# Windowed attention: scores in plain fp32 on 64x64 pieces over three blocks of 64 keys, and the value product on 64x64 pieces into two banks

## The reference

```python
q = l2norm(q) * qs
k = l2norm(k) * ksc
q, k = rotary_xpos(q, k)
...
bq = q.reshape(b, h, w, WINDOW, d) * QK_SCALE
bk, bv = (look_around(bk), look_around(bv))     # the window before, then the own window
sim = jnp.einsum('bhwid,bhwjd->bhwij', bq, bk)
mask = (i < j) | (i > j + WINDOW) | (j == -1)
sim = jnp.where(mask, -jnp.finfo(sim.dtype).max, sim)
attn = jax.nn.softmax(sim, axis=-1)
out = jnp.einsum('bhwij,bhwjd->bhwid', attn, bv)
```

## Time and profile before

| | |
|---|---|
| device time, median of 3 runs | 2664.02 us (2662.18 to 2664.52) |
| span of the profiled execution | 2660.9 us |
| PE / PEld / DVE / ACT / POOL busy | 98 / 87 / 83 / 67 / 60% of the span |
| mean granted TensorE clock | 0.999 of full speed |
| one sequence, from its first score product (565.22) to the next one's (640.66) | 75.4 us |

### The profile page before, as it was taken

How to read it: one execution, slowest core, us unless ns; L and a number is a source line. 1 busy time by engine, 2 the same in 40 slices (tenths; PEclk the granted TensorE clock), 3 DMA queues, 4 the chain that set the end, 5 groups by cost and what they waited for, 6 DMA issues and landing times.

```text
span 2660.9 us, 67491 instructions
## 1 busy us (share of the span) xinstructions
PE 2606.0 (98%) x23392; PEld 2307.9 (87%) x23392; DVE 2215.5 (83%) x6597; ACT 1777.2 (67%) x4872; POOL 1588.3 (60%) x1767
## 2 busy tenths in 40 slices
PE   8999999999999999999999999999999999999999
PEld 7888888888888888888767888888888988988888
DVE  8888888888888888888656888888888889888887
ACT  6677677666676666666454767666666666666665
POOL 6666666656666666665213666666666666666655
PEclk9999999999999999999999999999999999999999
DMA  3122111003000000005101000000003100000000
GB/s 120 34 81 77 38 29 53 22 20 116 14 2 2 2 2 25 2 2 200 34 18 33 2 2 2 2 2 2 2 2 116 34 2 18 18 18 18 17 18 25
DMA packets 75904, 81.38 MB, mean 31 GB/s; under 512 B 37552, under 2 KB 61872, under 8 KB 74416
## 3 DMA queue, kind: packets, MB, share of 16 engines
q1 hardware_dynamic: 70176, 75.51, 8.7%
q10 hardware_dynamic: 5392, 1.56, 0.2%
HBM read 49.53 MB, written 26.74 MB: 29 GB/s over the span
## 4 chain that ended last, share of the span: by engine, by line
PE 73%; DVE 14%; issue 5%; ACT 4%; POOL 4%; DMA 1%; SPq 0%; DVEq 0%; POOLq 0%; ACTq 0%
PE bank L1064 13%; PE bank L1066 12%; PE bank L1065 12%; PE bank L1271 9%; PE bank L1159 5%; PE bank L1124 5%; PE bank L1145 5%; PE bank L1100 4%; POOL pr L611 3%; PE bank L1432 2%; DVE t L1603 2%; DVE t L1600 2%; DVE pr L1638 2%; DVE h L1710 1%; ACT pr L792 1%
## 5 line engine op out<-in xcount | busy, mean ns | idle before, releaser
L611 POOL TENSOR_TENSOR pr<-pr,rden 128x512 f32<-128x512 f32 (+1 forms) x512 | 473.6, 943 | 424.0 <-DVE rden L1647 423.5
L792 ACT ACTIVATE pr<-pr,nb 128x256 f32<-128x256 f32 (+1 forms) x1024 | 479.1, 470 | 301.2 <-DVE nb L1638 301.2
L1638 DVE CUSTOM_DVE_ANT_0 pr<-bank,maskb,r 128x256 f32<-128x256 f32 (+1 forms) x1024 | 401.3, 445 | 20.7 <-PE bank L1124 8.7
L1064 PE MATMUL bank<-h2T,w 128*128 128x256 f32 x1408 | 408.2, 290 | 6.0 <-DVE qT L1624 1.0
L1065 PE MATMUL bank<-h2T,w 128*128 128x256 f32 x1408 | 395.0, 281 | 0.0
L1066 PE MATMUL bank<-h2T,w 128*128 128x256 f32 x1408 | 394.7, 280 | 0.0
L643 POOL TENSOR_TENSOR uTl<-t,uTh 128x256 fp32r<-128x256 f32 x288 | 219.3, 762 | 216.2 <-ACT uTh L868 215.4
L1728 DVE SCALAR_TENSOR_TENSOR t<-bank,b,t 128x256 f32<-128x256 f32 (+1 forms) x384 | 184.6, 481 | 159.6 <-ACT t L853 118.2
L1064 PE MATMUL bank<-wqkv,hT 128*128 128x512 f32 x768 | 303.7, 396 | 2.4 <-DVE nb L1638 2.4
L1065 PE MATMUL bank<-wqkv,hT 128*128 128x512 f32 x768 | 303.1, 395 | 0.0
L1066 PE MATMUL bank<-wqkv,hT 128*128 128x512 f32 x768 | 301.5, 393 | 0.0
(11 more groups left out here) (237 smaller groups left out, 7061.0 us busy)
## 6 DMA issues: line engine op xcount, KB each, us to landing
wqkv<-wqkv_split SPq DMA_DIRECT2D x18, 512.0 KB, 6.4
w<-w_split SPq DMA_DIRECT2D x3, 2816.0 KB, 10.6
Y<-in_x SPq DMA_DIRECT2D x8, 512.0 KB, 6.6
out<-Y SPq DMA_DIRECT2D x8, 512.0 KB, 3.9
stt<-stt SPq DMA_DIRECT2D x224, 3.0 KB
h<-out SPq DMA_DIRECT2D x7, 512.0 KB, 3.9
out<-h SPq DMA_DIRECT2D x7, 512.0 KB, 2.9
stt<-stt SPq DMA_DIRECT2D x192, 0.0 KB
```

Source lines behind the costliest of these rows:

```text
L611: e.tensor_tensor(pr[:, 2 * j:2 * j + 2, 0:wide], pr[:, 2 * j:2 * j + 2, 0:wide], rden[:, 2 * j:2 * j + 2].unsqueeze(2).to_broadcast([P, 2 ...
L792: last = e.activation(pr[:, hd, 0:wide], pr[:, hd, 0:wide], ACT.Exp, bias=nb[:, hd:hd + 1], scale=-1.0, accum_out=den[:, hd:hd + 1])
L1064: e.matmul(out, left[0], right[0], start=first, stop=False)
L1638: m = e.tensor_tensor_reduce(pr[:, hd, 0:wide], bank[j][:, g * 256:g * 256 + wide], far, r[:, t, 1, place(hd):place(hd) + 1], FAR, ALU.add ...
```

## The change

Tokens of a tile are seen in two halves of 64, and keys in blocks of 64. A query half sees 129 of at most three blocks, so scores, mask, exponential and normalisation are 192 wide for 256 (tiles 1 to 3); tile 0 stays 128 wide. The scores are one plain fp32 product for each piece, with no low parts: `kT` and `qT` are single, `A2_k` and `A2_q` go. Each product takes 64 rows (a head) by 64 columns (a query half) of the array; `kT` holds the eight key blocks in falling order. Per tile there are 24 calls (32 in tile 0), and the keys' order differs between the two heads of a pair and the two query halves. The pair lies side by side in 384 columns of `pr`: the outer two times 128 columns are the main parts, the 128 in the middle hold the edge parts of both heads. So a pair takes 3 transposes of 128 x 128 for 4: 8 for the main parts (`PT`) and 4 for the edge parts (`PTE`), 12 for 16.

The value product works on 64 x 64 pieces: the lower 64 keys of a block pair go to bank 6, the upper 64 to bank 3, so two sums lie in two banks. ScalarE copies the first (`O_first`), VectorE adds the second (`O_add`), into `o_sum`, which takes the place of the queries' low part; high and low part of the result are then made from `o_sum`. `A0` moves ahead of `O` on ScalarE and VectorE, and `fill(2)` behind `A2` on TensorE. `cuts` is new; in tile 0 five W2 products come ahead of the scores, where three stood between their halves. Apart from that, the last product of W2 uses 106 rows for 42.

```diff
-        maskb = sb("maskb", [P, 2, 2, WINDOW], BF16)
+        maskb = sb("maskb", [P, 4 * WINDOW], BF16)
-        qT = sb("qT", [P, HL, PAIRS, P], F32R)
+        qT = sb("qT", [P, HL, PAIRS, P])
+        o_sum = qT[:, 1, :, :].rearrange("p a c -> p (a c)")
-        kT = sb("kT", [P, HL, PAIRS, 2, P], F32R)
+        kT = sb("kT", [P, PAIRS, BLOCKS, HB])
+        def wide(t):
+            return 3 * HB if t else 2 * HB
+        def probs(j, t):
+            pr_j = pr[:, j, 0:6 * HB]
+            return cut(pr_j, 2) if t else cut(pr_j, 3)[:, ::2, :]
...
+            def PTE(L, b, t):
+                n = idx(L, b, t)
+                e.wait_ge(pt_ps, at(pt_ps, 3 * n + 3))
+                halves_of = bank[E_BANK][:, :].rearrange("p (u a c) -> p u a c", u=HEADS // 2, a=2)
+                for a in pair:
+                    for g in pair:
+                        last = e.activation(pTe[64 * a:64 * a + 64, g::2, :], halves_of[64 * g:64 * g + 64, :, a, :], ACT.Copy)
+                last.then_inc(pt_sb, 1)
+            def O_first(L, b, t):
+                n = idx(L, b, t)
+                e.wait_ge(o_lo, at(o_lo, 2 * n))
+                e.wait_ge(pv_ps, at(pv_ps, 2 * n + 2))
+                for i in pair:
+                    cols = slice(2 * P * i, 2 * P * i + 2 * P)
+                    e.activation(o_sum[:, cols], bank[O_BANK[0]][:, cols], ACT.Copy).then_inc(o_first, 1)
...
+                own = BLOCKS - 1 - 2 * t
+                if t:
+                    keys = ((((0, own, 3),), ((0, own, 2), (2, own - 1, 1))), (((1, own, 2), (0, own + 2, 1)), ((0, own - 1, 3),)))
+                else:
+                    keys = ((((0, own, 1), (1, own - 1, 1)),) * 2,) * 2
                 for s_ in range(2):
                     p = 2 * half + s_
+                    for g in range(2):
+                        rows = slice(64 * g, 64 * g + 64)
+                        for a in range(2):
+                            out = cut(bank[2 * half + g][64 * a:64 * a + 64, s_ * 256:s_ * 256 + 256], 4)
+                            for to, block, w in keys[s_][a]:
+                                m = e.matmul(out[:, to:to + w, :], qT[rows, 0, p, HB * a:HB * a + HB], kT[rows, p, block:block + w, :],
+                                             start=True, stop=True, skip_group_check=True)
...
+            def PTE(L, b, t, more):
+                n = idx(L, b, t)
+                if t < NT - 1 or more:
+                    e.wait_ge(v_sb, at(v_sb, n + 2))
+                for j in range(HEADS // 2):
+                    mm = e.transpose(bank[E_BANK][:, j * P:(j + 1) * P], pr[:, j, P:2 * P], ident[:, :])
                 mm.then_inc(pt_ps, 1)
...
+                for j in range(HEADS // 2):
+                    if j % 2 == 0:
+                        e.wait_ge(pt_sb, at(pt_sb, 3 * n + j // 2 + 1))
+                    for g in range(2):
+                        for a in range(2):
+                            mm = product(j, g, a, t - 1 if t and a else t, pTm, 0, j == 0, t == 0 and j == 3)
+                if t:
+                    e.wait_ge(pt_sb, at(pt_sb, 3 * n + 3))
+                    for j in range(HEADS // 2):
+                        for g in range(2):
+                            for a in range(2):
+                                mm = product(j, g, a, t if a else t - 1, pTe, HB * a, False, j == 3)
...
-                        rows = (64 + REST, REST)[i]
+                        rows = 64 + REST
...
-                    cuts = ((0, 9, 12, 12, UNITS), (0, 14, 14, 14, UNITS), (0, 14, 14, 14, UNITS), (0, 11, 11, 11, UNITS))[t]
+                    cuts = ((5, 9, 12, 14, UNITS), (0, 6, 11, 14, UNITS), (0, 6, 11, 14, UNITS), (0, 6, 11, 11, UNITS))[t]
...
+            def O_add(L, b, t):
+                n = idx(L, b, t)
+                for i in pair:
+                    cols = slice(2 * P * i, 2 * P * i + 2 * P)
+                    e.wait_ge(o_first, at(o_first, 2 * n + i + 1))
+                    e.tensor_tensor(o_sum[:, cols], bank[O_BANK[1]][:, cols], o_sum[:, cols], ALU.add).then_inc(o_added, 1)
...
+                    O_add(L, b, t)
+                    if ahead2:
+                        A0(*ahead2)
                     O(L, b, t)
                     if t == 3:
                         H2T(L, b, 0)
-                    if ahead2:
-                        A0(*ahead2)
-                    if ahead:
-                        A2_k(*ahead)
-                    if ahead and t < 3:
-                        A2_q(*ahead)
```

More of the change, by code:

```diff
@@ L1143, in PT @@
                 for g in range(2):
-                    for w in range(2 if t else 1):
-                        mm = e.transpose(bank[bk][:, (2 * g + w) * P:(2 * g + w + 1) * P],
-                                         pr[:, 2 * j + g, w * P:(w + 1) * P], ident[:, :])
+                    mm = e.transpose(bank[PT_BANK[a]][:, (2 * (j % 2) + g) * P:(2 * (j % 2) + g + 1) * P],
+                                     pr[:, j, 2 * g * P:(2 * g + 1) * P], ident[:, :])
+                if j % 2:
+                    mm.then_inc(pt_ps, 1 if t or a == 0 else 2)
@@ L1147, in PT, with PV, product @@
+            def PTE(L, b, t, more):
[4 more added lines that the diff above has]
+                    mm = e.transpose(bank[E_BANK][:, j * P:(j + 1) * P], pr[:, j, P:2 * P], ident[:, :])
                 mm.then_inc(pt_ps, 1)
-            def PV(L, b, t, j):
+            def PV(L, b, t):
                 n = idx(L, b, t)
-                if j == 0:
-                    e.wait_ge(xa_done, at(xa_done, n))
-                e.wait_ge(pt_sb, at(pt_sb, 4 * n + j + 1))
-                for g in range(2):
+                e.wait_ge(xa_done, at(xa_done, n))
+                def product(j, g, a, tile, right, lo, first, last):
@@ L1155, in PV @@
                     hd = 2 * j + g
-                    ws = (0, 1) if t else (0,)
-                    for w in ws:
-                        tile = t if w == t % 2 else t - 1
-                        mm = e.matmul(bank[O_BANK[j // 2]][64 * g:64 * g + 64, j % 2 * P:(j % 2 + 1) * P],
-                                      v[:, tile, hd * DH:(hd + 1) * DH], pT[:, hd, w, :],
-                                      start=(w == 0), stop=(w == ws[-1]))
-                if j % 2:
-                    mm.then_inc(pv_ps, 1)
+                    return e.matmul(bank[O_BANK[a]][64 * g:64 * g + 64, j * P + lo:j * P + lo + right.shape[-1]],
+                                    v[64 * a:64 * a + 64, tile, hd * DH:(hd + 1) * DH], right[64 * a:64 * a + 64, hd, :],
+                                    start=first, stop=last, skip_group_check=True)
@@ L1165, in WO @@
+                mm.then_inc(pv_ps, 2)
             def WO(L, b, t):
@@ L2110, in constants @@
     tab = tab.reshape(NT, P, 4, DH).transpose(1, 0, 2, 3).reshape(P, -1)
-    i, j = np.arange(P)[:, None], np.arange(2 * WINDOW)[None]
-    own = np.where(j[:, :WINDOW] > i, f(FAR), f(0))
-    before = np.where(j[:, :WINDOW] < i, f(FAR), f(0))
-    mask = np.concatenate([own, before, before, own], 1)
+    i, j = np.arange(P)[:, None], np.arange(HB)[None]
+    low, i = i < HB, i % HB
+    above, below = np.where(j > i, f(FAR), f(0)), np.where(j < i, f(FAR), f(0))
+    none = np.zeros((P, HB), f)
+    near, back, edge = np.where(low, above, none), np.where(low, none, below), np.where(low, below, above)
+    mask = np.concatenate([near, back, edge, edge, near, back, near, np.where(low, f(FAR), above)], 1)
     r_, c_ = np.arange(P)[:, None] % 64, np.arange(64)[None]
```

130 lines of the change are left out of this document (56 added, 74 removed).

## The result

| | before | after |
|---|---|---|
| median of the runs | 2663.8 us (4 runs, 2662.2 to 2664.5) | 2702.0 us (4 runs, 2701.0 to 2703.8) |
| profiled execution, its span | 2660.9 us | 2700.6 us |
| TensorE busy in the span | 98% | 94% |
| VectorE busy in the span | 83% | 77% |

A forecast was written before the change was run, and what follows sets the result against it. VectorE's chain to the projection, with only 0.30 us of slack, was taken to bound the kernel despite TensorE's 98%. Tiles 0 to 3 summed +0.6 + 0.1 + 0.1 - 0.6 = +0.2; x32 = +6.4, less 2.4: 2668 us, range 2625 to 2700.

The forecast's parts named there:

- To the first exponential: VectorE loop, from its first score operation to the first exponential: 0.80 us instead of 0.93, from two narrower score operations.
- to the squares: VectorE loop, from first exponential to sum of squares: 4.14 us instead of 4.57, from eight narrower exponentials.
- rotations: VectorE loop, squares and rotations up to the attention output's new work: 5.05 us, unchanged.
- 10.6 as the point from which it counts: Value product ending later than about 10.6 us after the scores' start would make ScalarE's bank 6 copy delay VectorE.
- Two additions, hT and low half: VectorE after the rotation: three operations of 0.33 us ahead of a 0.42 us low half, 1.41 against 0.42.
- 0.06 to the projection: Handover from VectorE's finished low half to the start of TensorE's output projection: 0.06 us.
- Projection to its reader: From the output projection's start to VectorE's operation that reads it: about 1.6 us, then 1.36 to the next scores.
- Tile 0, +0.6: One-window tile: no narrower softmax, only the new work on VectorE's chain, so 0.6 us longer per sequence.
- Tile 3, -0.6: Last tile, to the feed-forward part: narrower GpSimd normalisations bring the squares 1.2 us earlier; 14.55 us for 15.10.
- rival 1: GpSimd truly holds tile 3, its relief is larger: squares at about 4.9 instead of 5.82, 2639 us; chance 0.25.
- TensorE's terms: In two-window tiles: scores some 1.6 us (0.2 less), transposes 0.44 less, value product 1.7 (0.3 less); 0.9 less altogether.
- Rival 2: Four-piece instructions cost 26.5 ns or more whatever their columns, so the value product ends at 10.8; 2690 us, chance 0.23.

## Why the prediction was wrong

The direction was given 0.37, the time lay 2 us outside the range. The mechanism was the forecast's own: TensorE's gain is worth nothing, because VectorE's chain to the projection doesn't get shorter (without the sum the kernel is 114 us faster; without the edge products nothing changes). Its price was too low, step by step:

- To the first exponential 0.80 (measured 665.49 - 664.69 = 0.80), to the squares 4.14 (669.63 - 665.49 = 4.14), rotations 5.05 (5.09). Right. The 0.04 may be ScalarE's copy out of bank 6, 10.66 after the scores' start; I had 10.6 as the point from which it counts.
- Two additions, hT and low half, 1.41, and 0.06 to the projection, 1.47 together: measured 1.94 in tile 1, of it 0.38 the hold-up by GpSimd, and 1.56 in the other tiles. **This is the step that failed most**: I took the low half's duration from one that reads PSUM and asked neither what its new source is nor what GpSimd does beside it. Taking the collision away gave 14.7 us of the 34 missing.
- The remaining 1.55 is seen in tile 0 as well: there the first low half is done at 661.56 and the projection starts 0.14 later, not 0.06. Before, the projection hardly ever waited for it, so no row showed a real handover; I took one that was hidden. 0.08 x 4 x 32 = 10 us.
- Projection to its reader, "about 1.6": measured 1.69. The three numbers in my own line give 1.50 - 0.12 + 0.28 = 1.66, which I rounded down, and it was 668.18 - 666.48 = 1.70 before. From there to the scores 1.31 for 1.36. Together 0.04 x 128 = 5 us.
- Tile 0, +0.6: measured +0.70 in the median, which is the handovers. Three of the first nine sequences took 1.6 to 2.2 us more than before instead of 0.7: in two of them TensorE stood for 0.8 us in the W2 products that now go ahead of the scores, the third is not explained. In the sequence whose tile 1 is shown above, the rotation's last addition (L1661) took 0.88 us instead of 0.69, with GpSimd's normalisation of the keys ending 0.33 into it; in the kernel before, the latter ended 0.02 ahead of it. That happened in 4 sequences.
- Tile 3, -0.6: to the projection -0.26, to the start of the feed-forward part -0.55. Right: the squares come 5.76 after the first score operation, where I had 5.82 and rival 1 had 4.9, and behind a layer norm operation and not ScalarE, so rival 1 falls. But I left the feed-forward part out of the sum as unchanged. Its last layer norm operation is now held up beside GpSimd in 18 of 32 sequences: 18 x 0.54 = 10 us. In half of the others, projection and feed-forward part take 0.5 less than before; on the whole 0.25 us of the forecast's gain is missing in each sequence.
- TensorE's terms: scores 1.6 (1.61), transposes 0.44 less, value product 1.7 (1.84, of which some 0.3 is a wait for ScalarE's copies of the edges). Right, and worth nothing.
- Rival 2, the small products' pace, had the right sign with the wrong cause. The rule that spoke for it doesn't hold here: the 32 edge records started at 673.48 and the next transpose at 674.11, under 20 ns each with the change of shape in it. The row from the trace:

```profile
673.48 0.69 PE L1201 MATMUL bank<-pT,v 64*64 64x64 f32 x32
674.11 0.33 PE L1113 MATMUL bank<-ident,Y 128*128 128x128 f32 x1
```

The Trainium skill's floor (TensorE: Matmul & The Clock Gate, Part 1) would be 0.8 us for them (an estimate from the page). On four pieces at a time the measurement decides against it.

These steps overlap. By place, as means over the sequences of the two profiled executions (tile 0 without the passes that don't follow directly on another), the change against the forecast: tile 0 +0.79 for +0.58, tile 1 +0.57 for +0.09, tile 2 +0.25 for +0.09, tile 3 with the feed-forward part -0.30 for -0.55. That is 0.21 + 0.48 + 0.16 + 0.25 = 1.10 us for each sequence, 35 us in all, against 34 missing. The range failed because its upper end held one mechanism (rival 2 with an error) and not a chain that is longer at each handover and meets GpSimd in two places. That the time lay only 2 us outside is luck: the range reached so far up for rival 2, which did not happen.

## What to carry to other kernels

Before a sum goes over two banks because the array's pieces work at the same time, count the detour that it puts on the path, handover by handover; writing in turns may cost a fraction of it. An operation whose source moves from PSUM to SBUF is another operation: look at what GpSimd does beside it, before and after the shift that the change itself makes. Look at it in the stages that the change doesn't edit, too: in the feed-forward part a hold-up of 0.54 us came with a shift of less than 0.1 us. And work saved ahead of a wait for another engine is given back at that wait; the wait need not be the next one in the program, nor the one that comes to mind.

## What the runs showed of the hardware

- VectorE's subtraction with two operands in SBUF (128 x 256) took 0.79 us for 0.42 when GpSimd's sum of two SBUF tiles had started 0.22 before it, in 30 of 32 sequences; with that sum moved behind it, 0.41 to 0.43 in all 256 cases. Beside GpSimd operations on 8 columns (L622) it wasn't held, nor was the same subtraction with one operand in PSUM beside GpSimd's sum (60 cases, at most 0.43).
- A VectorE operation with a 128 x 128 tile in SBUF as its source (L1760) took 0.87 us for 0.33 in 18 of 32 cases, with a subtraction of GpSimd that started 0.06 to 0.07 after it. In the other 14 it took 0.33 to 0.34, most of them with GpSimd as close behind.
- The rotation's operations that read a bank took 0.68 to 0.69 with GpSimd beside them.
- 64 score records of 64 columns took 1.35 us with the change of shape, 21 ns each; 32 value products of 64 columns 0.63 us, 20 ns each, so the small products on four pieces go faster than the 26.5 ns of the earlier trace rows.
- A projection that waited for VectorE started 0.14 us after the low half's end; VectorE to ScalarE took 0.09, ScalarE to VectorE 0.06.
- After a 42-row product the row-pair scores started 0.08 us later, scores on 64x64 pieces 0.31; after a 106-row product 0.21.
